# An expert-layer kernel: VectorE adds the second expert's row to each output piece of the last batch

## The reference

```
scores = softmax(mask @ G);  value, indices = top_k(scores, 2)
gate = silu(mask @ gate_w);  up = mask @ up_w
out  = sum over the token's 2 experts of w * ((gate * up) @ down_w)
out  = out + sum over the same 2 of w * (mask @ lora_A) @ lora_B
return x + out
```

## Time and profile before

| what | us |
|---|---|
| median of three runs | 780.76 |
| profiled execution, whole | 781.71 |
| its span in the trace | 780.0 |
| busy: PE / DVE / ACT / POOL | 492.1 / 524.0 / 449.7 / 389.1 |
| last batch's tiles, about | 622 to 746 |
| after the last tile | 746 to 780 |

### The profile page before, as it was taken

How to read it: one execution, slowest core, us unless ns; L and a number is a source line. 1 busy time by engine, 2 the same in 40 slices (tenths; PEclk the granted TensorE clock), 3 DMA queues, 4 the chain that set the end, 5 groups by cost and what they waited for, 6 DMA issues and landing times.

```text
span 780.0 us, 13619 instructions
## 1 busy us (share of the span) xinstructions
PE 492.1 (63%) x3682; PEld 328.7 (42%) x3682; DVE 524.0 (67%) x1242; ACT 449.7 (58%) x655; POOL 389.1 (50%) x337
## 2 busy tenths in 40 slices
PE   0311177259878882877878829787769188797900
PEld 0310066246544551654545516454446155464500
DVE  5768789877587788955986888558843624343245
ACT  5688268849854575686445666874337155464400
POOL 7114200045366222787787237878861178777500
PEclk9855589769999995898999959999889789999965
DMA  9990070013313373478367825773776248767479
GB/s 313 364 288 6 0 270 3 26 41 116 116 63 116 115 278 101 156 237 281 113 227 255 337 95 168 258 272 117 243 261 266 83 148 296 241 224 255 149 278 379
DMA packets 76984, 147.29 MB, mean 189 GB/s; under 512 B 21475, under 2 KB 30699, under 8 KB 76400
## 3 DMA queue, kind: packets, MB, share of 16 engines
q1 hardware_dynamic: 59248, 104.40, 39.3%
q0 software_dynamic: 17664, 41.98, 14.8%
HBM read 95.47 MB, written 69.21 MB: 211 GB/s over the span
## 4 chain that ended last, share of the span: by engine, by line
PE 20%; DVE 17%; DMA 17%; POOL 15%; issue 14%; ACT 7%; DVEq 5%; SPq 2%; POOLq 1%; ACTq 0%
PE pa L692 7%; DMA out_dram<-piece 5%; DMA piece<-put_rows 4%; DMA xg<-mask_rows,where 4%; ACT mask L807 4%; POOL piece L540 3%; DVE mask L1077 3%; POOL piece L543 3%; POOL put_rows L531 2%; POOL xg L523 2%; DMA w<-put_rows 2%; DVE small L1039 2%; PE pc L715 1%; DMA v<-in_x_dram 1%; PE pc L718 1%
## 5 line engine op out<-in xcount | busy, mean ns | idle before, releaser
L692 PE MATMUL pa<-w,xt 128*128 x1472 | 200.4, 290 | 5.2 <-issue 4.3
L692 PEld LDWEIGHTS pa<-w,xt 128*128 128x128 f16 x1472 | 146.4, 100 | 65.6 <-issue 17.3
L523 POOL DMA_INDIRECT xg<-mask_rows,where x92 | 100.5, 1093 | 114.4 <-DVEq L1351 92.8
L531 POOL DMA_INDIRECT put_rows<-y,where x92 | 92.3, 1003 | 129.9 <-ACT y L864 109.1
L864 ACT ACTIVATE y<-pc,where 128x512 f32<-128x512 f32 x184 | 125.1, 688 | 52.2 <-PE pc L718 51.9
L851 ACT ACTIVATE xt<-pb 128x1024 f16<-128x1024 uint8 x92 | 93.9, 1021 | 88.0 <-PE pb L679 88.0
L1359 DVE SCALAR_TENSOR_TENSOR g_full<-pa,where,s_act 128x144 f32<-128x144 f32 x92 | 33.5, 364 | 155.6 <-ACT s_act L856 155.4
L856 ACT ACTIVATE s_act<-pa,small 128x128 f32<-128x128 f32 x92 | 33.7, 367 | 97.2 <-PE pa L692 97.2
L679 PE MATMUL pb<-ident,xg 128*128 128x128 f16 x368 | 38.9, 233 | 75.5 <-DMA xg<-mask_rows,where 57.3
L715 PE MATMUL pc<-wd,gt 128*128 x184 | 75.4, 410 | 0.1
L716 PE MATMUL pc<-wd,gt 128*128 x184 | 75.4, 410 | 0.0
(11 more groups left out here) (208 smaller groups left out, 873.6 us busy)
## 6 DMA issues: line engine op xcount, KB each, us to landing
piece<-put_rows SPq DMA_DIRECT2D x96, 256.0 KB, 3.9
v<-in_x_dram SPq DMA_DIRECT2D x40, 512.0 KB, 8.6
piece<-in_x_dram SPq DMA_DIRECT2D x48, 256.0 KB, 2.7
out_dram<-piece SPq DMA_DIRECT2D x48, 256.0 KB, 3.7
w<-put_rows SPq DMA_DIRECT2D x16, 512.0 KB, 9.6
w<-in_L_ffn_gate_w_dram SPq DMA_DIRECT2D x8, 512.0 KB, 10.4
w<-in_L_ffn_up_w_dram SPq DMA_DIRECT2D x8, 512.0 KB, 8.4
wd<-in_L_ffn_down_w_dram SPq DMA_DIRECT2D x8, 512.0 KB, 9.5
```

The source lines that it names most:

```text
L523: pool.indirect_dma_start(out=xg[:, g % NX, :], out_offset=None, in_=mask_rows[n % 2], in_offset=bass.IndirectOffsetOnAxis(ap=mask_row[n][ ...
L531: pool.indirect_dma_start(out=put_rows[n % 2], out_offset=bass.IndirectOffsetOnAxis(ap=put_row[n][:, i:i + 1], axis=0), in_=y[:, g % NY, : ...
L692: last = pe.matmul(l1[g % 2], xt[:, g % 2, t, :], w1[:, bass.ds(e, 1), t, k, :].rearrange("p o n -> p (o n)"), start=(t == 0 and k == 0), ...
```

## The change

In the last batch's rounds, GpSimd returns after the first of the two adds of a piece, and a new VectorE function `end_sum` does the second. VectorE calls it at the end of round i, behind `gate(i)` and `store_gt(i-1)`, for the piece that `PIECE_AT` names for that round. It waits for GpSimd's first add of the piece and for the piece's transfers, and releases SyncE's store. The pieces of batches 0 and 1, which are added during batches 1 and 2, are handled as before.

```diff
@@ sum_piece, GpSimd
                 nc.gpsimd.tensor_tensor(piece[:, at, 0, :], piece[:, at, 0, :], piece[:, at, 1, :],
                                         ALU.add).then_inc(half_summed, 1)
+                if n == B - 2:
+                    return
                 pool.wait_ge(half_summed, u + 1)
@@ VectorE
+            def end_sum(n, j):
+                u = PIECES * n + j
+                at = u % NC
+                dve.wait_ge(half_summed, u + 1)
+                dve.wait_ge(piece_landed[at], 48 * (u // NC + 1))
+                V.tensor_tensor(piece[:, at, 0, :], piece[:, at, 0, :], piece[:, at, 2, :],
+                                ALU.add).then_inc(summed_piece, 1)
@@ VectorE, loop over the tiles
                     if i >= 1:
                         store_gt(n, i - 1)
                     between(i, 2)
+                    if not more and i in PIECE_AT:
+                        end_sum(n - 1, PIECE_AT[i])
```

## The result

| | us |
|---|---|
| predicted | 777.5 (774.6 to 780.7) |
| measured, median of 20 runs | 785.97 (782.01 to 788.98) |
| before, median of 20 runs beside them | 780.66 |
| ratio to before, 95% interval | 1.0061 (1.0044 to 1.0078) |

The ratio leaves out executions in the chip's slower state (one of the kernel before here, at 806 us) and is not the quotient of the medians. The time lies outside the range, and the sign was wrong: I gave 0.09 to slower, and the rival that I had named for it is not what happened.

The account below looks back on a forecast made before the run. The bound was taken to be the two-buffer loop of load, adds and store. Stretches of -0.8 and -2.5 us, 0.1 given back, made -3.2: 778.5 for the profiled execution, 777.5 for the median, range 774.6 to 780.7.

Parts of the forecast that it names:

- the rival that I had named for it: At the pieces' stores: VectorE's add held up by GpSimd's adds, 1.96 us each, +3.2 in all, 784.0; chance 0.08.
- What bounds the kernel: Rounds with pieces: a two-buffer loop of load, land, two adds, store, land; 11.83 us a turn, 5.9 a piece against TensorE's 4.0.
- the held gate: The next tile's gate, queued on VectorE behind the waiting add: costed at nothing, with 3.5 us to spare.
- The add, 0.69 us: The second add on VectorE, 512 columns: 0.69 us, bounds 0.61 and 1.96.
- The start: Rounds 1 and 2: piece 0's add on VectorE ends 3.76 us late, making piece 2's first add 1.6 to 2.3 late.
- I take the other buffer to start as late: Start of the odd buffer: assumed as late as the even one, whose piece 2 first add is 1.6 to 2.3 us late.
- A turn 0.6 shorter: Each turn of a buffer: landing to store 1.98 us in place of 2.60, so 0.6 shorter while VectorE stands ready.
- the half microsecond that I had named as a sign of being wrong: Pieces' landings: the prediction is wrong if they grow by half a microsecond.
- the rival that I gave 0.12: Buffer turns: transfers stretch by 5%, 0.45 us a turn, taking back 2.25 of the 3.2; 779.8; chance 0.12.
- The gather 1.34 sooner: GpSimd's gather follows the first add by 1.41 us in place of 2.75; counts once at each stretch's end.
- The held add: The same rival: VectorE's add held up beside GpSimd's adds, deciding from 1.3 us an add on; 784.0; chance 0.08.
- The sum: Whole last batch: -0.8 from the first stretch, -2.5 from the second, 0.1 given back for handovers: -3.2 us.

Follow-up runs that it names:

- the four-buffer run: Kernel before with four buffers in place of two for the last batch's pieces, SyncE storing piece j-3 before loading piece j, both adds on GpSimd: 773.24 us, 0.9899.
- the two runs with its steady rounds and an early start: The change, with pieces 0 and 1 added wholly on GpSimd (781.92 us, 1.0006), or their VectorE adds moved ahead of gate or copy (782.38 us, 1.0019).
- the second profile of before: The unchanged kernel profiled once more for spread: 786.37 us, last batch 124.0 us from first gather to last put, against 122.2 in its first profile.
- the first two experiments: VectorE makes the second add of pieces 2 to 15 only (781.92 us, 1.0006), then of pieces 0 and 1 only (785.15 us, 1.0066); GpSimd makes the rest.
- the run with pieces 0 and 1 alone: VectorE makes the second add of pieces 0 and 1 only, GpSimd both adds of pieces 2 to 15: 785.15 us, 1.0066 to the kernel before.
- stores from ScalarE: Two buffers, VectorE's second adds of pieces 2 to 15, last-batch stores issued by ScalarE: 782.26 us, 1.0015; repeated with 0 and 1 stored by SyncE: 780.83, 1.0009.
- the two with four buffers and VectorE's adds: Four buffers in the last batch, VectorE making the second add of pieces 2 to 15 (768.22 us, 0.9811) or of all 16 (767.83 us, 0.9835).

## Why the prediction was wrong, step by step

*What bounds the kernel*: right. The loop through two buffers was the bound; the four-buffer run shows it, and the held gate cost nothing (TensorE waited 0.5 us for line 1369, once, as it had for line 1367 before).

*The add, 0.69 us*: right, 0.68 to 0.69.

*The start*: mis-sized, and this is the loss. I had piece 2's first add late by 1.6 to 2.3; it was 3.8. The store was late by 4.3 and not 3.76; it took 2.7 to land in place of 2.0, so the load was late by 5.0; and of the 7.1 us that I took for 1.45 to 2.16 to spare, landing took 5.9 (634.12 to 640.00). "I take the other buffer to start as late" was worse still: piece 1's store left behind the load of piece 2 and took 5.28 to land (635.45 to 640.73), and the first add of piece 3 came at t = 29.7 in place of 24.3, +5.4.

*A turn 0.6 shorter*: failed. The adds gave about 0.4 of it with the change (first add to store 2.29, 2.64 to 2.68 where GpSimd makes both adds), but store to next load grew to 4.71 (3.8 to 4.1 there), more than the half microsecond that I had named as a sign of being wrong. A turn is 12.4 with the change, 11.8 in the two runs with its steady rounds and an early start, against 12.0 to 12.2 with GpSimd's adds. The three turns of the first stretch that were to win back the start won nothing: piece 8's first add was at t = 59.6 in place of 54.7, +4.9 (+3.4 beside the second profile of before). My loop had SyncE waiting for the sum; with the shorter add SyncE waits for stores to land instead. This is the rival that I gave 0.12, the transfers taking it back; I had priced it together with a start that cost 2 and not 4 to 5. Why the stores land later when they are asked for sooner stays open.

*The gather 1.34 sooner*: it does follow the first add by 1.41, but its issue takes 0.45 longer (below), so 0.9 is left at its end, once a stretch.

*The held add* (the slower rival): wrong as a mechanism. No add took over 0.69. The slower case came by the start, a term that I had in the sum with the right sign and half its size, and had left with 0.01 as a cause of slower.

*The sum*: I had a start of about +2, less 1.8 and 1.2 in turns, less the gathers. Measured in the last batch: +3.8 to +5.4 at pieces 2 and 3, and +5.9 at the last put, with nothing won in between (+3.1 to +4.7 and +4.1 beside the second profile of before). In this one profile TensorE's rounds 12 to 16 also took 4.2 to 4.6 us in place of 4.0, partly idle in what the profile calls issue; in the first two experiments most of them take 4.0. I have no cause for it. It, or the spread of 1.8 between the two profiles of before, may make up the difference between 5.9 here and 4.8 in the runs.

## What to carry to other kernels

When an operation moves to another in-order engine, look first at the rounds in which a loop is filled, not at its steady turn: what stands ahead of it there? A lateness at the start of a loop that is the bound can stay to the end: it did in the change and in the run with pieces 0 and 1 alone, and was won back in part with stores from ScalarE. And before shortening a step of a ring of buffers, compare its share with the transfers' (2.6 of 12 us here): where a load waits for a store issued just before it, more buffers were worth more here (1%) than a faster step (nothing that could be told), and only then did the faster step count (another 0.5 to 1%).

## What the runs showed of the hardware

A gather's issue on GpSimd takes 1.04 us, but 1.48 to 1.49 where VectorE's add of two SBUF inputs has begun just before it. In the changed kernel eleven gathers did so, among them the one at 666.15, 0.12 after an add; one that began before VectorE's add did not:

```profile
694.37 1.04 POOL L523 DMA_INDIRECT xg<-mask_rows,where  x1 [0.16 <-issue]
```
```profile
694.59 0.68 DVE L1384 TENSOR_TENSOR piece<-piece 128x512 f32<-128x512 f32 x1
```

In the profiles in which GpSimd makes both adds of pieces 2 to 15 no gather took over 1.18, and in the two with four buffers and VectorE's adds, where each gather began before the add, none took over 1.05. I had taken the add and the gather to lie beside each other freely. The Trainium skill ("SBUF — State Buffer", section "Who interferes with whom") infers that such an add does not hold up the issue of a gather. The measurement decides: the add's own 0.69 isn't stretched, the gather's issue is, by 0.45. The 0.31 that I had taken as agreeing was an add that began 0.8 into a gather (649.92, the gather at 649.12), the order in which neither is held. Which part of the issue is held is not shown.
